# The stage before the first softmax phase of a gated cross-attention and mixture-of-experts kernel, written in another order

## The reference, cut to what matters

```python
x = x + tanh(g_xattn) * xattn(layernorm(x), ctx, ctx, ...)     # x, ctx: (8, 256, 512)
x = x + tanh(g_ffn) * moe(layernorm(x), ...)                   # 8 experts, top 2

def xattn(query, key, value, encoding, Wq, bq, ...):
    q = proj(Wq, bq, query).reshape(b, HD, H, n)               # D = 256 channels, 16 heads of 16, n = 512
    k = proj(Wk, bk, key).reshape(b, HD, H, n)
    v = proj(Wv, bv, value).reshape(b, HD, H, n)
    q, k = rope(encoding, q), rope(encoding, k)                # t * f0 + rotate_half(t) * f1
    prob = softmax(einsum('bdhn,bdhm->bhnm', q, k) / sqrt(HD))
    return proj(Wm, bm, einsum('bhnm,bdhm->bdhn', prob, v))
```

## Time and profile before

| | us |
|---|---|
| three runs | 1095.29, 1096.87, 1099.82 (median 1096.87) |
| the profiled execution | 1096.43 |
| its span | 1094.6 |
| TensorE busy | 1045.0 (95%) |
| VectorE busy | 801.2 (73%) |
| ScalarE busy | 669.6 (61%) |
| GpSimd busy | 384.0 (35%) |

### The profile page before, as it was taken

The page is one execution under the profiler, slowest core; times in us unless marked ns, Lnnn a source line. Parts: engine busy times, 40 slices in busy tenths (PEclk is TensorE's granted clock), DMA queues, the critical chain, the costliest instruction groups (busy, mean ns, idle before and its releaser), DMA issues. The chain is left out here.

```text
span 1094.6 us, 18879 instructions
## 1 busy us (share of the span) xinstructions
PE 1045.0 (95%) x5894; PEld 422.9 (39%) x5894; DVE 801.2 (73%) x1643; ACT 669.6 (61%) x921; POOL 384.0 (35%) x491
## 2 busy tenths in 40 slices
PE   7998999999999999998988999999999999999997
...
GB/s 203 124 105 192 185 111 198 118 95 110 78 114 156 97 81 108 98 124 101 98 175 196 227 155 160 209 134 219 91 137 210 138 189 113 221 152 77 63 56 49
DMA packets 182223, 149.65 MB, mean 137 GB/s; under 512 B 122672, under 2 KB 144176, under 8 KB 182128
## 3 DMA queue, kind: packets, MB, share of 16 engines
...
...
## 5 line engine op out<-in xcount | busy, mean ns | idle before, releaser
L1545 PE MATMUL psum<-W,xs 128*128 128x512 f16 x1824 | 398.5, 380 | 4.2 <-DMA xs<-xs 2.2
L627 ACT ACTIVATE W<-psum,es 128x512 f32<-128x512 f32 x512 | 319.8, 690 | 75.5 <-PE psum L388 73.0
L879 DVE TENSOR_REDUCE MX<-psum 128x2 f32<-128x1024 f32 x256 | 308.3, 1218 | 39.9 <-PE psum L377 38.4
L1545 PEld LDWEIGHTS psum<-W,xs 128*128 128x128 f16 x1824 | 177.4, 98 | 223.8 <-issue 9.2
L388 PE MATMUL psum<-stg 50*128 50x512 f16 x512 | 166.8, 387 | 20.5 <-DVE ON L905 8.3
L1819 POOL DMA_INDIRECT out<-xs,target x34 | 53.1, 1562 | 278.6 <-ACT xs L726 278.3
L377 PE MATMUL psum<-stg 48*128 48x512 f16 x512 | 142.7, 382 | 2.1 <-DMA stg<-scr 1.0
L1675 DVE TENSOR_TENSOR xs<-xs,psum 128x512 f32<-128x512 f32 x68 | 46.2, 685 | 129.6 <-ACT xs L711 129.6
L401 PE MATMUL psum<-W 128*32 128x512 f32 x1024 | 138.1, 612 | 0.0
L711 ACT ACTIVATE xs<-psum,i 128x512 f32<-128x512 f32 x68 | 46.1, 680 | 131.7 <-PE psum L1545 105.7
L752 DVE SCALAR_TENSOR_TENSOR W<-stg,scw,W 128x1024 f16<-128x1024 f32 x96 | 117.3, 1278 | 8.9 <-ACT W L738 8.6
...
## 6 DMA issues: line engine op xcount, KB each, us to landing
...
```

The costliest lines, as they stand in the source:

```text
L627: act.activation(m.Pb[:, c % 2, hh, :], m.home(tile), ACT.Exp, scale=m.es[:, hb // 2:hb // 2 + 1]).then_inc(S["exped"], 1)
L879: dve.tensor_reduce(m.MX[:, hb % 2, c0:c0 + 9:8], m.psS[tile % 2], AX_X, ALU.max, negate=True).then_inc(S["maxed"], 1)
L1545: return pe.matmul(out, rows, m.wh[(e % 2, w)][:, wp, cols], start=start, stop=stop)
```

## The change

- **Loads.** ScalarE issues the biases, the flattened rope constants `fx`, the sign, the q and k parts of wT, the swap matrix and the v part of wT. SyncE issues x, ctx, `fT`, then x and ctx of batch item 1 without a wait, then the eleven small tensors, then x of batch item 2.
- **Scales.** The reduction over the partitions is split in two: six columns, then ctx's. The first q and k scales are worked out operation by operation side by side.
- **ScalarE** multiplies `fT` by the sign and casts the upper parts of head batch 0. VectorE turns with three operations each and subtracts afterwards. It takes the statistics of tiles 2 and 3 ahead of that, those of 4 and 5 in phase -1.
- **Rows.** Pair p = 0 of head batch 0 goes from `q12` to `stk` within SBUF (`stack_near`), 12 transfers over both queues. The other three pairs go through DRAM as before. Scores of pair 0 wait for `near` only.
- **Jobs.** k of head batch 1 is projected in phase -1; q of head batch 2 moves from step 0 to 6, the second v from 6 to 10, the second k of phase -1 from 10 to 13. SyncE and the waits follow.
- **Maxima of ctx** of batch item 1 go by `far_write` and `far_read`; its k scale moves from step 3 to step 6.
- **GpSimd** fills `stk`'s constant rows one ring place at a time, the last and the ones in `vT` behind the rope of head batch 1.

```diff
-        return [("q", 0), ("k", 0)] if s == 0 else []
+        return [("k", 0), ("q", 0)] if s == 0 else []
     if ph == -2:
-        return [("q", 1), ("k", 1)] if s == 0 else []
+        return [("q", 1)] if s == 0 else []
     if ph == -1:
-        return {0: [("q", 2)], 3: [("v", 0)], 6: [("v", 1)], 9: [("m", 0)], 10: [("k", 2)]}.get(s, [])
+        return {0: [("k", 1)], 3: [("v", 0)], 6: [("q", 2)], 9: [("m", 0)], 10: [("v", 1)], 13: [("k", 2)]}.get(s, [])
...
+SECOND = {1: ("k", 1), 4: ("v", 0), 7: ("q", 2), 11: ("v", 1), 14: ("k", 2)}
 
...
-            pe.wait_ge(S[f"stk{hb % 3}{w}"], 96 * nth(hb, 3))
+            if hb == 0:
+                pe.wait_ge(S["near"], 192)
+            if hb or p:
+                pe.wait_ge(S[f"stk{hb % 3}{w}"], 96 * nth(hb, 3))
...
+    far = 0 if hb else 1
     for j, part in enumerate((0, 0, 1) if w == 0 else (0, 1, 0)):
         heads = m.scr[hb % 2, w, part].rearrange("(p u d) n -> u d p n", u=2, d=16)
         for u in us:
             r = 64 * u + 16 * j
-            eng.dma_start(m.stk[hb % 3][r:r + 16, w, :, :], heads[u]).then_inc(S[f"stk{hb % 3}{w}"], 16)
+            eng.dma_start(m.stk[hb % 3][r:r + 16, w, far:4, :], heads[u][:, far:4]).then_inc(S[f"stk{hb % 3}{w}"], 16)
+
+
+def stack_near(eng, m, S, w, part, u):
+
+    if part == 0:
+        eng.wait_ge(S["high"], w + 1)
+    else:
+        eng.wait_ge(S[f"roped{w}"], 1)
+    eng.wait_ge(S["const_rows"], 1)
+    for j in range(3):
+        if ((0, 0, 1), (0, 1, 0))[w][j] == part:
+            r = 64 * u + 16 * j
+            eng.dma_start(m.stk[0][r:r + 16, w, 0, :], m.q12[16 * u:16 * u + 16, w, part, :]).then_inc(S["near"], 16)
...
-    load(m.wT, "wT", "wT")
-    for dst, nm in ((m.bq, "bq"), (m.fx, "fx"), (m.fT, "fT"), (m.swap, "swap"), (m.sgn, "sgn")):
-        load(dst, nm, "rope_in")
+    load(m.bq, "bq", "wT")
+    load(m.fx, "fx", "wT")
+    load(m.sgn, "sgn", "rope_in")
+    act.dma_start(m.wT[:, 0:2], io["wT"][:, 0:2]).then_inc(S["wT"], 16)
+    load(m.swap, "swap", "rope_in")
+    act.dma_start(m.wT[:, 2:3], io["wT"][:, 2:3]).then_inc(S["rope_in"], 16)
     root(1, 0, 2)
...
-    for kind, i in jobs_at(-3, 0):
-        job(kind, i)
-    act.wait_ge(S["small"], 64)
-    act.wait_ge(S["router"], 16 * 7)
+    act.wait_ge(S["rope_in"], 64)
+    act.activation(m.fT[:, 1, :], m.fT[:, 1, :], ACT.Identity, scale=m.sgn[:, 0:1]).then_inc(S["signed"], 1)
+    job("q", 0)
+    job("k", 0)
+    root(2, 2, 4)
+    act.wait_ge(S["turned"], 1)
+    act.copy(m.q12[:, 0, 0, :], m.qb[:, 0, :]).then_inc(S["high"], 1)
+    stack_near(act, m, S, 0, 0, 1)
+    act.wait_ge(S["turned"], 2)
+    act.copy(m.q12[:, 1, 0, :], m.qb[:, 1, :]).then_inc(S["high"], 1)
+    stack_near(act, m, S, 1, 0, 1)
+    stack_near(act, m, S, 0, 1, 1)
+    stack_near(act, m, S, 1, 1, 1)
+    job("q", 1)
+    act.wait_ge(S["router"], 16 * 11)
     act.activation(m.tg2[:, :], m.gf[:, :], ACT.Tanh).then_inc(S["tg"], 1)
     act.activation(m.tg[:, :], m.gx[:, :], ACT.Tanh).then_inc(S["tg"], 1)
-    job("q", 1)
     stack(act, m, S, 0, 0, (1,))
-    root(2, 2, 6)
     stack(act, m, S, 1, 0, (1,))
-    job("k", 1)
...
+                if ph == -1 and s == 4:
+                    for w in range(2):
+                        act.wait_ge(S[f"stk0{w}"], 96)
+                    load_ctx(act, m, S, io, 2)
+                if ph == -1 and s == 12:
+                    stack(act, m, S, 1, 1, (1,))
+                    root(3, 4, 6)
+                    act.activation(m.warm[:, 0:1], m.epst[:, :], ACT.Exp)
...
     def spread(ph, s):
-        if ph == -1 and s == 3:
-            k_scale(1)
+        if ph == -1 and s == 8:
+            stats(4, 6)
+            variances(4, 6)
+        if ph == -1 and s == 14:
+            dve.wait_ge(S["std"], 3)
+            dve.reciprocal(m.rstd[:, 4:6], m.rstd[:, 4:6]).then_inc(S["rstd_near"], 1)
...
+        if ph % 2 and 1 <= b < NB and s == (6 if b == 1 else 4):
+            dve.wait_ge(S["far_read"], 16 * b)
...
+            dve.wait_ge(S["far_largest"], b)
             k_scale(b)
...
-        scale(0, 22.65).then_inc(S["first_scales"], 1)
-        scale(1, m.bigs[:, 6:7]).then_inc(S["first_scales"], 1)
...
+        dve.wait_ge(S["largest_of_all"], 2)
+        step.more(dve.tensor_scalar(m.bound[:, 1:2], m.byx[:, 1:2], m.bigs[:, 6:7], m.byb[:, 1:2], ALU.mult, ALU.add))
+        step.settle()
+        for n in range(2):
+            step.more(dve.tensor_scalar(m.p2[:, n:n + 1].bitcast(I32), m.bound[:, n:n + 1].bitcast(I32), 0x7F800000, None, ALU.bitwise_and))
...
+        for n in range(2):
+            dve.tensor_scalar(m.sbias[:, n, 0:1], m.bq[:, n, 0:1], m.sc[:, n:n + 1], None, ALU.mult).then_inc(S["first_scales"], 1)
...
+    def first_turned(w):
+
+        p, f = m.psum[:, SWAPPED[w], :], m.qb[:, w, :]
+        evacuated(dve, S, ("qk"[w], 0))
+        dve.wait_ge(S["rope_in"], 64)
+        step.more(dve.tensor_tensor(m.qs[:, w, :], f, m.fT[:, 0, :], ALU.mult))
+        dve.wait_ge(S[f"swapped{w}"], 32)
+        dve.wait_ge(S["signed"], 1)
+        step(dve.tensor_tensor(p, p, m.fT[:, 1, :], ALU.mult))
+        dve.tensor_tensor(f, m.qs[:, w, :], p, ALU.add).then_inc(S["turned"], 1)
+
+    def first_lower(w):
+        dve.wait_ge(S["turned"], w + 1)
+        dve.wait_ge(S["high"], w + 1)
+        dve.tensor_tensor(m.q12[:, w, 1, :], m.qb[:, w, :], m.q12[:, w, 0, :], ALU.subtract).then_inc(S[f"roped{w}"], 1)
...
     stats(0, 2)
     variances(0, 2)
-    dve.wait_ge(S["wT"], 16)
-    step.more(dve.tensor_reduce(m.big[:, 0:2], m.wT[:, 0:2, :, :].rearrange("p w i o -> p w (i o)"), AX_X, ALU.max, apply_absolute_value=True))
+    largest()
     inverse(1, 0, 2)
+    largest_weights()
     norm(dve, m, S, 0)
-    largest()
+    ctx_rows(m.big[:, 6:7], 0).then_inc(S["largest"], 1)
     first_scales()
-    dve.tensor_scalar(m.fT[:, 1, :], m.fT[:, 1, :], m.sgn[:, 0:1], None, ALU.mult).then_inc(S["signed"], 1)
+    stats(2, 4)
+    variances(2, 4)
+    first_turned(0)
+    first_turned(1)
+    first_lower(0)
+    first_lower(1)
+    inverse(2, 2, 4)
+    norm(dve, m, S, 1)
     ctx_rows(m.big[:, 7:8], 1).then_inc(S["ctx_rows_largest"], 1)
-    rope_steps(dve, step, m, S, 0, 0)
-    rope_steps(dve, step, m, S, 1, 0)
-    stats(2, 6)
-    variances(2, 6)
-    dve.wait_ge(S["std"], 2)
-    dve.reciprocal(m.rstd[:, 2:6], m.rstd[:, 2:6]).then_inc(S["rstd_near"], 1)
-    dve.wait_ge(S["rstd_near"], 1)
-    norm(dve, m, S, 1)
...
-    pool.memset(m.vT[:, :, :, :, 16:32], 1.0).then_inc(S["const_ones"], 1)
-    pool.wait_ge(S["const_ones"], 1)
+
+    const_rows(0)
...
-    pool.wait_ge(S["largest"], 1)
-    pool.partition_all_reduce(m.bigs[:, 0:7], m.big[:, 0:7], 128, bass.bass_isa.ReduceOp.max).then_inc(S["largest_of_all"], 1)
-    pool.wait_ge(S["largest_of_all"], 1)
-    pool.wait_ge(S["ctx_rows_largest"], 1)
-    pool.partition_all_reduce(m.bigs[:, 7:8], m.big[:, 7:8], 128, bass.bass_isa.ReduceOp.max).then_inc(S["ctx_largest"], 1)
-    pool.wait_ge(S["ctx_largest"], 1)
+    for n in range(2):
+        v = slice(6 * n, 6 + n)
+        pool.wait_ge(S["largest"], n + 1)
+        pool.partition_all_reduce(m.bigs[:, v], m.big[:, v], 128, bass.bass_isa.ReduceOp.max).then_inc(S["largest_of_all"], 1)
+        pool.wait_ge(S["largest_of_all"], n + 1)
...
+    const_rows(1)
...
+            if ph == -2 and w:
+                const_rows(2)
+                pool.memset(m.vT[:, :, :, :, 16:32], 1.0).then_inc(S["const_rows"], 1)
+                pool.wait_ge(S["const_rows"], 4)
...
     load_x(sp, m, S, io, 0)
     load_ctx(sp, m, S, io, 0)
-    sp.wait_ge(S["rope_in"], 80)
+    load(m.fT, "fT", "rope_in")
     load_x(sp, m, S, io, 1)
     load_ctx(sp, m, S, io, 1)
...
     load_x(sp, m, S, io, 2)
+    stack_near(sp, m, S, 0, 0, 0)
+    stack_near(sp, m, S, 1, 0, 0)
+    stack_near(sp, m, S, 0, 1, 0)
+    stack_near(sp, m, S, 1, 1, 0)
     keep(0, 0)
+    keep(1, 0)
     swap(0, 1)
-    keep(1, 0)
+    far_write(1)
     stack(sp, m, S, 0, 0, (0,))
     stack(sp, m, S, 1, 0, (0,))
+    far_read(1)
     swap(1, 1)
     keep(0, 1)
     stack(sp, m, S, 0, 1)
+    keep(1, 1)
+    max_rows(0)
+    stack(sp, m, S, 1, 1, (0,))
     swap(0, 2)
-    keep(1, 1)
-    stack(sp, m, S, 1, 1)
-    max_rows(0)
     swap(1, 2)
     keep(0, 2)
     max_rows(1)
```

More of the change, by code:

```diff
@@ L317, in project_out @@
         evacuated(pe, S, ("b", 2 * b + 1))
-        pe.wait_ge(S["small"], 16 * 4)
+        pe.wait_ge(S["router"], 16 * 11)
         for t in range(2):
@@ L458, in tensor_attention @@
         if ph == -1:
-            early(20)
+            early(16)
         for st in range(8):
@@ L484, in tensor_attention @@
                 if ph == -2 and s == 0:
+                    early(3)
                     swap_first(0)
@@ new lines, in first_scales @@
+        step.more(dve.tensor_scalar(m.byb[:, :], m.bigs[:, 2:4], m.F[:, 0:1], 1e-30, ALU.mult, ALU.add))
+        step.settle()
+        step.more(dve.tensor_scalar(m.bound[:, 0:1], m.byx[:, 0:1], 22.65, m.byb[:, 0:1], ALU.mult, ALU.add))
```

(13 more changed lines are left out.)

103 lines of the change are left out of this document (51 added, 52 removed).

## The result

Changed kernel 1111.38 us (median of 4, 1107.8 to 1112.37), kernel before 1097.91 (1095.29 to 1099.82): ratio 1.0113, 95% interval [1.0092, 1.0134]. The forecast was 1098.7. The profiled execution has a span of 1110.4 us and a mean granted clock of 0.978 (before 0.991).

What follows compares the result with a forecast made beforehand. TensorE's expert loop ends last, so only what the opening still saves when the attention ends counts; 1096.43 + 0.3 (q of batch 3) + 1.5 (clock) = 1098.2, 1098.7 with the median's 0.44; range 1091 to 1102.

Steps and rivals of the forecast that it cites:

- Loads and scales: Opening: x at 4.5, wT at 7.1, `largest` full at 11.4, q evacuated at 13.4 instead of 15.09.
- rival 3: Opening loads: x and ctx of batch 1, issued early, delay wT and what follows by 2.7 us; 1101.4, chance 0.10.
- Turning: VectorE's turning of the first q and k: the last subtraction ends at 21.6, where it was 24.27.
- Rows without DRAM: Near rows sent SBUF to SBUF land in 2.0 us; first score at 24.5, 7.7 us earlier.
- Pair 4 onward: Other heads' DRAM copy: written at 23.2, 7.9 us as upper bound, rows at 31.1, fifth reduction at 32.0; 6.9 left.
- VectorE, 1.5 + 1.4: Phase of the first scores: k scale with a reduction adds 1.5, statistics of tiles 4 and 5 add 1.4; 3.9 left.
- SyncE's order: Swap of q of batch 2 behind maxima rows, issued at 46.6; q of batch 3 evacuated at 56.4, +0.3, gain gone.
- Clock, +1.5: TensorE stops some 4 us after phase 0 starts; the lower clock behind that wait costs 1.5 us, bounds 0 and 2.5.
- Rival 4: Batch 1's ctx maxima through DRAM: SyncE stands until they land, later swap slips, low clock twice; 1103.1, chance 0.12.
- Rivals 1 and 2: Opening's head start: 3.9 us survives, 1093.0, chance 0.20; or all 7.7 survive, 1089.2, chance 0.08.

Runs made afterwards that it cites:

- e6_hold: e3_both, but SyncE issues the loads of x1 and ctx1 only once wT has landed; 1102.42 us.
- e1_gp: Changed kernel without the small write: maxima of ctx of batch item 1 are again reduced over the partitions on GpSimd; 1104.43 us.
- e3_both: e1_gp with the swap of q of head batch 2 issued ahead of the first maxima rows, as before; 1100.47 us.
- c1_sbfar: Changed kernel, all items' ctx maxima collected into one SBUF row before DRAM, item 1's row and read back issued later; 1104.65 us.
- c2_before: Kernel before, zero rows' transfers moved behind phase 1's x load, maxima of items 2 to 7 collected through a row of SBUF; 1093.38 us.
- c5_all: e3_both with zero rows' transfers moved, TensorE's jobs beside the first scores reordered, maxima of items 2 to 7 through a row of SBUF; 1094.69 us.

## Why the prediction was wrong

Point by point, with the terms of its sum.

- **Loads and scales**: half right. x was there at 5.00 (I said 4.5), wT at 9.96 (7.1), q evacuated at 15.74 (13.4). 0.9 us of it is rival 3, by e6_hold. Most of the rest is size, by an estimate: in e6_hold x, ctx, fT and wT, 2.36 MB, were all but alone and wT was waited for until 9.14 still; at the 394 GB/s of the earlier trace rows that is 6.0 us of transfer. I had left ctx and fT, issued by SyncE beside it, out of the sum.
- **Turning**: 7.3 us from q's evacuation to the end of the last subtraction (15.74 to 23.08), where I had 8.2.
- **Rows without DRAM**: right in kind. From the last subtraction (23.08) to the first score 3.9 us, where it was 7.9; I had 2.9. First score 26.98 for 24.5.
- **"Pair 4 onward"**: this is the step that failed. I took the 7.9 us of before as an *upper* bound for the copy through DRAM and put the rows at 31.1, the fifth reduction at 32.0. They were 38.67 and 39.32. The bound was read from a stretch with no small write in it. Without the write (e1_gp) that reduction is at 34.45, 2.5 us late, about as much as the first score. So the small write, which the sum left out of this term, cost 4.9 us at this step, and 3.0 more up to `mT` (14.1 us from the fifth reduction instead of e1_gp's 11.1): behind TensorE's stop of 4.90 us the granted clock was 0.50 from 39 to 45.
- **VectorE, 1.5 + 1.4**: 0.8 too small. In e1_gp it is 11.1 us from the fifth reduction (34.45) to `mT` (45.56), where I had 7.4 + 2.9.
- `mT`: forecast 42.3, measured 53.41. Of the 11.1 us, 7.8 are the write (53.41 less 45.56), 2.5 the head, 0.8 VectorE.
- **SyncE's order**: the path right, its price not. From `mT` to q of batch 3 14.4 us (I took 14.1); GpSimd began 3.8 us behind the swap's issue at 58.05 (I took 3.9), and the evacuation at 67.84 followed the end of its rope at 67.75. But I set this against the 9.9 us of before. TensorE's own path had meanwhile grown from 9.9 to 13.1 (e3_both, with the order of before), by the 3.2 us that phase 0 began later behind `mT`. So at this evacuation the order cost 1.4 us and not 4.2 (by the medians of e1_gp and e3_both it cost 4 in the end); that the 14 us came out is partly luck.
- **Clock, +1.5**: too small. From q's to k's evacuation 11.8 us instead of 9.4, with a granted clock of 0.74 from 67 to 80; TensorE's next stop was 5.11 us instead of 3.31, 1.4 more by then. And the sum priced one such wait: behind the 2.31 us before `mT`, which it did not have, the granted clock was 0.50 as well.
- **Rival 4** had the place and the landing: 8.0 us, `far_read` at 35.24, the swap behind it at 35.68 (36.1 in the text). It priced only SyncE's standing still, 1103.1. What the earlier trace rows showed was read as the latency of one transfer; while such a transfer is under way the others are slow too, the fifth pair's reads among them. It got 0.12.

Rivals 1 and 2 stay unproved: no run kept more than 1.9 us at `mT` (e6_hold 44.67, c1_sbfar 44.37), and those two did not end under the kernel before.

Still open: why the versions on the changed kernel, with the write, the order, the zero rows and the jobs put right, end level with or behind c2_before, although their first score is 5 us earlier. In c5_all the lead over c2_before is 5.0 us at the first score and 0.5 at `mT` (45.08 and 45.59). Between them stand VectorE's added work and a granted clock of 0.64 from 28 to 32; no run took either away alone.
